# The last group's dense products: four stretches of five units in place of seven of up to three

## The reference

```
xn = layernorm(x)
q  = rope(xn @ wq + bq)          # 32 heads of 16
k  = rope(xn @ wk + bk)          # 8 key heads of 16, each serves 4 query heads
v  = xn @ wv + bv                # 8 value heads of 16
s  = softmax(q k^T / 4) v        # per head, 1024 x 1024 scores
z  = xn @ W^T + b                # 512 x 512, the "dense" product
m  = sum over 8 experts of p_e * (xn @ A_e) @ B_e      # rank 16 each, 128 in all
gamma = min(0.5 * |z| / (|m| + 1e-6), 1)               # norms per token
g  = silu(z + gamma * m)
out = x + s * g
```

## Time and profile before

| | |
|---|---|
| median of 3 runs | 428.94 us (428.89 to 430.34) |
| the profiled execution: its time, its span | 429.27 us, 427.4 us |
| PE busy | 416.1 us, 97% |
| DVE busy | 371.0 us, 87% |
| ACT busy | 310.2 us, 73% |
| POOL busy | 157.8 us, 37% |
| the last group (scores of L1197 on PE) | from 375.6 us to the end |

### The profile page before, as it was taken

The page is one execution under the profiler, slowest core; times in us unless marked ns, Lnnn a source line. Parts: engine busy times, 40 slices in busy tenths (PEclk is TensorE's granted clock), DMA queues, the critical chain, the costliest instruction groups (busy, mean ns, idle before and its releaser), DMA issues.

```text
span 427.4 us, 8367 instructions
## 1 busy us (share of the span) xinstructions
PE 416.1 (97%) x3179; PEld 185.9 (43%) x3179; DVE 371.0 (87%) x613; ACT 310.2 (73%) x612; POOL 157.8 (37%) x215
## 2 busy tenths in 40 slices
PE   7999999999999999999999999999999999999994
PEld 3647433343444344444444443444444443454441
DVE  6744798998999999999999999999999999933653
ACT  2232011227889998998989998999999999976884
POOL 7972322446003130403042044324431454501565
PEclk9999999999999999999999999999999999999999
DMA  8949995544000020000000000000000000002002
GB/s 266 305 113 126 132 133 75 74 77 74 4 0 3 2 59 3 2 2 2 4 2 2 2 3 5 2 2 2 3 2 3 2 3 2 5 2 88 21 23 68
DMA packets 13624, 18.09 MB, mean 42 GB/s; under 512 B 3168, under 2 KB 7552, under 8 KB 13584
## 3 DMA queue, kind: packets, MB, share of 16 engines
q1 hardware_dynamic: 12064, 16.44, 20.3%
q10 hardware_dynamic: 1520, 1.12, 1.0%
HBM read 6.72 MB, written 2.10 MB: 21 GB/s over the span
## 4 chain that ended last, share of the span: by engine, by line
PE 84%; DVE 5%; POOL 3%; DMA 2%; issue 2%; ACT 2%; SPq 1%; DVEq 0%; POOLq 0%; ACTq 0%
PE st L1161 31%; PE oT L1129 27%; PE st L969 6%; PE oT L1218 3%; PE sm L1243 3%; PE oT L969 3%; PE sm L1073 2%; DVE neghalf L838 2%; PE sm L1138 2%; DMA x_sb<-in_x 2%; PE sm L1048 2%; PE st L1197 2%; PE st L998 2%; POOL arena L487 1%; DVE negmax L830 1%
## 5 line engine op out<-in xcount | busy, mean ns | idle before, releaser
L838 DVE TENSOR_REDUCE neghalf<-sm 128x1 f32<-128x512 f32 x448 | 270.9, 682 | 1.0 <-PE sm L1048 0.7
L744 ACT ACTIVATE arena<-st 128x512 f32<-128x512 f32 x448 | 233.3, 600 | 22.0 <-PE st L1161 17.3
L1048 PE MATMUL sm<-kA,qA 48*128 48x512 f32 x448 | 156.7, 442 | 0.3 <-DVE neghalf L838 0.2
L1161 PE MATMUL st<-qA,kA 50*128 50x512 f32 x448 | 153.0, 438 | 0.5 <-ACT arena L744 0.2
L1129 PE MATMUL oT<-arena,vg 128*32 128x256 f32 (+3 forms) x1568 | 128.5, 419 | 0.0
L1161 PEld LDWEIGHTS st<-qA,kA 50*128 50x128 f32 x448 | 73.1, 184 | 96.8 <-ACT arena L744 81.8
L558 POOL TENSOR_TENSOR rsum<-junk,consts 128x16 f32<-128x16 f32 x13 | 37.9, 2914 | 103.1 <-ACT junk L716 103.1
L1048 PEld LDWEIGHTS sm<-kA,qA 48*128 48x128 f32 x448 | 73.2, 184 | 3.5 <-DVE neghalf L838 2.3
L1129 PEld LDWEIGHTS oT<-arena,vg 128*32 128x32 f32 x1568 | 33.4, 108 | 46.2 <-issue 41.5
L830 DVE TENSOR_REDUCE negmax<-sm 128x1 f32<-128x1024 f32 x32 | 37.9, 1217 | 7.0 <-PE sm L1073 7.0
L644 ACT ACTIVATE arena<-arena 128x512 fp32r<-128x512 f32 x7 | 4.4, 630 | 40.9 <-POOL arena L487 40.9
(11 more groups left out here) (138 smaller groups left out, 394.5 us busy)
## 6 DMA issues: line engine op xcount, KB each, us to landing
qA<-arena SPq DMA_DIRECT2D x45, 128.0 KB, 5.1
x_sb<-in_x SPq DMA_DIRECT2D x8, 256.0 KB, 5.8
kA<-qA SPq DMA_DIRECT2D x12, 128.0 KB, 6.7
wT_sb<-in_wT SPq DMA_DIRECT2D x1, 1024.0 KB, 7.5
out<-x_sb SPq DMA_DIRECT2D x1, 896.0 KB, 4.1
out<-x_sb SPq DMA_DIRECT2D x4, 224.0 KB, 1.9
z_sb<-in_wq SPq DMA_DIRECT2D x1, 768.0 KB, 10.0
qA<-qA SPq DMA_DIRECT2D x3, 128.0 KB, 3.8
```

Source lines behind the costliest of these rows:

```text
L744: act.activation(probs[:, s % PB, h, :], st[:, st_score(0, s, h) % 3, :], ACT.Exp, scale=float(D) ** -0.5).then_inc(st_free, 1)
L838: dve.tensor_reduce(neghalf[:, e // 16, e % 16, j % 2:j % 2 + 1], sm[:, n % 4, :], AX.X, ALU.max, negate=True).then_inc(sm_free, count)
L1048: pe.matmul(sm[:, n % 4, :], qA[rows, half, g // 2, h, qt * P:(qt + 1) * P], kA[rows, g // 2, kh * HALF:(kh + 1) * HALF], start=True, stop ...
L1161: pe.matmul(st[:, n % 3, :], kA[rows, g // 2, kt * P:(kt + 1) * P], qA[rows, half, g // 2, h, :], start=True, stop=True).then_inc(st_full, 1)
```

## The change

The table `LATE_UNITS` is written anew, nothing else. Before, rounds 0 to 6 had 3, 3, 3, 3, 3, 3 and 2 units, in the order of the tiles. Now rounds 0, 2, 4 and 6 have all five units of tiles 4, 5, 6 and 7, and rounds 1, 3 and 5 have none. The number of matmuls is the same.

```
-LATE_UNITS = {0: [(4, 0), (4, 1), (4, 2)], 1: [(4, 3), (4, NE), (5, 0)], 2: [(5, 1), (5, 2), (5, 3)],
-              3: [(5, NE), (6, 0), (6, 1)], 4: [(6, 2), (6, 3), (6, NE)], 5: [(7, 0), (7, 1), (7, 2)],
-              6: [(7, 3), (7, NE)]}
+
+LATE_UNITS = {2 * k: [(TH + k, c) for c in range(NE + 1)] for k in range(TH)}
```

## The result

The changed kernel took 433.48 us (median of 4 runs, 432.77 to 438.3) against 429.19 us of the kernel before (now four runs), a ratio of 1.0108 with a 95% interval of 1.0069 to 1.0148: slower. Two more sets, each beside the kernel before on one chip, gave 1.0125 (1.0082 to 1.0168) and 1.0098 (1.0059 to 1.0137). The forecast was 432.6 us. The profiled execution took 432.77 us with a span of 431.0, 3.5 us more than the profiled one of before (429.27), and the waits for the exponentials make that up. The median's distance is larger, 4.3 us, because two of the four executions were dearer (434.16 and 438.3 us); such executions are told of under the experiments.

The account below looks back on a forecast made before the run. PE bounds the kernel on average, with the exponentials setting a floor in rounds without dense work. 4.20 + 1.87 - 0.47 - 0.88 - 1.02 = +3.70 us on the median 428.94 gives 432.6 us, range 430.9 to 434.4.

Parts of the forecast that it names:

- The average that says PE is the bound: Whole kernel: PE busy 97% of the span, so moving its work within its own queue should cost nothing on average.
- The two paces: Last group: PE's 0.233 us a dense matmul plus 0.18 us a stretch, against ACT's 0.483 us between exponentials.
- The floor of 3.13 us: Least time from an even tile's first score to the values behind the odd tile, set by four banks and the exponentials.
- The long stretches: Rounds 0, 2, 4 and 6: fifteen dense matmuls take 3.68 us; +1.40 us each in the first three, +1.87 in round 6.
- Rounds 1, 3 and 5: Rounds left without dense matmuls give back only 1.02, 0.47 and 0.88 us, as the scores wait for exponentials.
- Nothing hidden elsewhere: Other engines' waits, bank claims and gates add nothing; 2.8 us of room in round 2, 0.65 left at the end.
- The waits' side effect on the clock: Rival: a new wait drops PE's clock from 2.4 to 1.2 GHz for the next round, 6.2 us more, 438.8 us; chance 0.04.
- exponentials that keep up: Rival: odd tiles' scores are not held, so each emptied round loses its whole 2.28 us; 428.2 us, chance 0.03.
- half-priced stalls: Rival: about half of the 4.2 us of new waits for exponentials is taken away; 430.6 us, chance 0.11.
- a late claim: Rival: a bank claim or gate comes late, DVE or POOL over 2.8 us later in round 2; 433.6 us, chance 0.07.

Follow-up runs that it names:

- the ring of five: Changed kernel with five banks for the scores in place of four, all z through one bank; lowest time 431.05 us, ratio 1.0044 to the kernel before.
- the halved exponentials: Both kernels with exponentials of tiles 2, 6 and 10 cut to half the columns; changed kernel's lowest time 430.13 us, kernel before at ratio 0.999.
- the 437.3 us execution: One profiled execution of the changed kernel, run again without further edits beside the kernel before to count executions; 437.3 us.
- the added matmuls: Changed kernel with twelve or 27 thrown-away dense matmuls more in rounds 1, 3 and 5; ratios to the kernel before 1.0073 and 1.0140.

## Why the prediction was right, and where it was not

The average that says PE is the bound: right on its own terms, and no help. The kernel became slower with PE's share unchanged.

The two paces: right. The floor of 3.13 us, read from tile 12 alone, came back in rounds 3 and 5 to a few hundredths, and the ring of five and the halved exponentials moved it by what they should.

The long stretches: 3.65 us measured, 3.68 taken. One start for a whole stretch was the right choice; units do not each pay one. The sum of the rounds, 3.6 us where 3.70 was forecast, is less by what the stretches are shorter.

Rounds 1, 3 and 5: right to 0.01 us, each from the end of a tile's last exponential plus 0.05 and 0.42 us.

Nothing hidden elsewhere: right. m's claims and the gates cost nothing, and the end behind tile 14's scores took 11.99 us in both.

The waits' side effect on the clock: wrong in its chance. Its price was about right (6.2 us for one whole round at the lower level; 4.4 us measured over four rounds in part of their time), but it got 0.04, from one execution's record, where five of 16 executions had it in this size. One of these five was profiled; the other four have mean clocks of 0.986 to 0.992. The forecast took round 1's wait of before, where the clock held, as a sign that it would hold; one execution in which it holds does not say how often it does. The Trainium skill's case, "TensorE: Matmul & The Clock Gate", section "A second HAM failure mode: psum-queue depth-cycling", in which short waits between groups of matmuls send the clock down and up again, fits what the 437.3 us execution shows: twice to 0.50, with 1.00 between.

Luck: the median lies 0.9 us above the forecast and inside the range because two of the four executions were undisturbed. In the next set, with three dear executions of six, it was 434.77 us, above the range. What the prediction's working gives is the undisturbed time: 427.4 + 3.70 + 1.87 = 432.97 us, where the profiled execution took 432.77.

The rivals: exponentials that keep up were refuted by the added matmuls and by the spread of tile 7's scores, half-priced stalls by the sum of the rounds; a late claim did not occur.

## What to carry to other kernels

Filler work beside a chain paced by another engine is worth most where it fills a wait: here no less than 3.13 us passed from a round's first score to its values, however little the round held, with a ring of four banks, so work that left a round gave back 0.5 to 1.0 us of its 2.3, and cost its full price where it went. Read the floor from the one place where the filler already is too short, and fill each round up to it and no further. Where PE must wait again and again, look at the granted clock of several executions before pricing the wait.

## What the runs showed of the hardware that was not expected

The clock can fall to 0.50 in waits that the profile hardly shows as idle: in the 437.3 us execution PE counts as busy for 7.90 of the 8.00 us from 376.0 to 384.0, ahead of the fall. It also fell where none of these waits stands: to 0.50 from 115.7 to 119.0 us in the run with shorter exponentials, after 3.6 us of which PE was busy for 3.31. It fell in some executions and not in others of the same kernel; what decides that stays open.
